# Two-layer network on one core: where the low parts of the hidden layers' activations are subtracted, and the written-out order

## The reference

```
x = layer0(x)
h = modulate(layernorm(x))
q, k, v = rope(h @ Wqkv);  x = x + gate_a * (softmax(causal(q k^T / 4)) v @ Wproj + b)
h = modulate(layernorm(x))                       # 512 x 256
z = silu(h @ w1^T * s1) * (h @ w2^T * s2)        # 512 x 1024: "up"
z = gelu(z @ h1^T * sh1)                         # 1024 -> 1024: "h1"
z = gelu(z @ h2^T * sh2)                         # 1024 -> 1024: "h2"
x = x + gate_b * (z @ w3^T * s3)                 # 1024 -> 256: "last"
```

## Time and profile before

| | |
|---|---|
| runs | 1975.2, 1977.19, 1977.64 us; median 1977.19 us |
| the profiled execution | 1979.78 us, of which the span from first to last instruction is 1978.0 us |
| mean granted PE clock | 0.971 |
| PE busy | 1856.4 us, 94% |
| DVE busy | 1375.4 us, 70% |
| ACT busy | 907.2 us, 46% |
| POOL busy | 510.0 us, 26% |

### The profile page before, as it was taken

How to read it: one execution, slowest core, us unless ns; L and a number is a source line. 1 busy time by engine, 2 the same in 40 slices (tenths; PEclk the granted TensorE clock), 3 DMA queues, 4 the chain that set the end, 5 groups by cost and what they waited for, 6 DMA issues and landing times.

```text
span 1978.0 us, 39009 instructions
## 1 busy us (share of the span) xinstructions
PE 1856.4 (94%) x15449; PEld 1293.8 (65%) x15449; DVE 1375.4 (70%) x2407; ACT 907.2 (46%) x1116; POOL 510.0 (26%) x597
## 2 busy tenths in 40 slices
PE   7998999899999998887999999999999999999998
PEld 4665657565666664444677676676776776776787
DVE  5667677766776677778768678587588678587443
ACT  2656574656565653332444524524534434534431
POOL 2434353443444342121211203102204003112120
PEclk8898999999999999888999999999999999999999
DMA  6221213221321110400122122221231231221321
GB/s 184 58 46 42 59 37 73 50 58 28 86 52 26 40 39 5 171 1 17 44 81 78 54 85 62 65 87 50 75 96 30 86 93 44 86 84 43 112 83 43
DMA packets 171812, 126.26 MB, mean 64 GB/s; under 512 B 113944, under 2 KB 148720, under 8 KB 171248
## 3 DMA queue, kind: packets, MB, share of 16 engines
q1 hardware_dynamic: 170800, 123.74, 22.6%
...
## 4 chain that ended last, share of the span: by engine, by line
PE 77%; DVE 15%; ACT 4%; issue 3%; POOL 1%; DMA 0%; SPq 0%; DVEq 0%; POOLq 0%; ACTq 0%
PE ps L2041 24%; PE ps L2025 5%; PE ps L1078 5%; PE ps L1922 4%; PE ps L1984 3%; PE ps L983 3%; PE ps L1952 3%; PE ps L2055 2%; PE ps L1108 2%; PE ps L1041 2%; PE ps L1130 2%; PE ps L1023 2%; DVE b_maxima L1689 2%; PE ps L1968 2%; PE ps L1964 2%
## 5 line engine op out<-in xcount | busy, mean ns | idle before, releaser
L2041 PE MATMUL ps<-b_acts,b_hidden_w 128*128 128x512 f32 x2048 | 504.6, 398 | 1.1 <-POOL b_acts L1616 1.1
L2041 PEld LDWEIGHTS ps<-b_acts,b_hidden_w 128*128 128x128 f32 x2048 | 376.2, 188 | 90.9 <-issue 9.8
L452 POOL TENSOR_SCALAR_AFFINE_SELECT a_probs<-a_probs 128x512 f32<-128x512 f32 (+1 forms) x224 | 166.3, 758 | 357.4 <-ACT a_probs L863 249.1
L1608 POOL TENSOR_SCALAR_AFFINE_SELECT b_work<-b_work 128x512 f32<-128x512 f32 x128 | 83.3, 663 | 673.1 <-ACT b_work L1843 673.0
L1879 ACT ACTIVATE b_acts_exact<-ps,c_s 128x512 f32<-128x512 f32 x128 | 88.2, 689 | 297.6 <-PE ps L2041 297.4
L863 ACT ACTIVATE a_probs<-ps 128x2048 f32<-128x2048 f32 (+1 forms) x96 | 153.2, 1595 | 123.5 <-DVEq L713 86.7
L1843 ACT ACTIVATE b_work<-ps 128x2048 f32<-128x2048 f32 (+1 forms) x96 | 153.4, 1597 | 90.8 <-PE ps L1968 89.0
L1689 DVE TENSOR_REDUCE b_maxima<-ps 128x4 f32<-128x2048 f32 (+3 forms) x128 | 187.9, 1489 | 3.3
L1787 DVE CAST b_acts<-b_acts_exact 128x512 fp32r<-128x512 f32 x128 | 55.8, 436 | 164.2 <-ACT b_acts_exact L1879 163.9
L1078 PE MATMUL ps<-a_probs,c_va 128*17 128x192 f32 (+4 forms) x2048 | 136.6, 388 | 2.9 <-issue 1.5
L1686 DVE TENSOR_TENSOR ps<-ps,c_causalr 128x512 f32<-128x512 f32 x128 | 86.1, 696 | 45.2 <-PE ps L1952 43.4
...
## 6 DMA issues: line engine op xcount, KB each, us to landing
b_hidden_w<-turned_h SPq DMA_DIRECT2D x128, 512.0 KB, 3.5
a_raw_next<-in_L_ffn_h_w SPq DMA_DIRECT2D x512, 16.0 KB, 1.8
...
```

The lines of the kernel that those rows point to most:

```text
L452: return nc.gpsimd.affine_select(out=z, in_=z, compare_op=ALU.is_ge, fill=0.0, base=0, pattern=[[0, blocks_n], [1, cols]], channel_multipl ...
L2041: ins = nc.tensor.matmul(here, view(hidden_w[:, m, k]), view(src[:, k, i]), start=(k + i == 0), stop=(k == NHID - 1 and i == 1))
```

## The change

Two things are edited. First, the subtraction of the low part of every hidden tile (`h1` and `h2`, 128 in all) moves from DVE to POOL. DVE's copy now adds to a new semaphore `h_high`; POOL waits for that count, subtracts, and adds to `h_split`. DVE's wait for its own copy goes. Second, `ORDER` is replaced by another order of the same 1750 entries: the first 357 entries and the last 53 (from `last.6.1.1` on) are the same, and what lies between is shuffled locally. In layer 0 no step changes; only its place in the order does.

```diff
@@ ORDER @@
-0:xT.2.1 0:lv.13.0 0:lin.14.0 0:lv.13.1 0:again.14 0:win.13.0 0:lh.12 0:r.2.0 0:lv.13.2 0:win.13.1 0:lv.14.0 0:win.14.0 0:norm.4 0:wv.13.0 0:kk.2.0
...
-1:h2.1.6.0 1:max.3.1.1 1:turn.2.1 1:h2.1.6.1 1:h2.1.7.0 1:max.3.1.2 1:h2.1.7.1 1:out.2.0 1:att.3.0.0 1:out.2.1 1:last.1.0.0 1:att.3.0.1 1:values.3.0.0
...
+1:max.3.1.0 1:heads.2.3 1:h2.1.5.1 1:h2.1.6.0 1:max.3.1.1 1:turn.2.1 1:h2.1.6.1 1:h2.1.7.0 1:again.3.0 1:max.3.1.2 1:h2.1.7.1 1:out.2.0 1:att.3.0.0
+1:out.2.1 1:last.1.0.0 1:att.3.0.1 1:values.3.0.0 1:last.1.0.1 1:xT.2 1:last.1.1.0 1:att.3.0.2 1:split.2 1:tq.3.2 1:last.1.1.1 1:up.2.0.0 1:tk.3.2
...
@@ second_layer @@
     h_split = sem("gelu_split")
+    h_high = sem("gelu_high_ready")
@@ gpsimd @@
                 nc.gpsimd.tensor_tensor(act_a[:, i, 1], exact_a[:, i], act_a[:, i, 0].bitcast(F32), ALU.subtract).then_inc(a_ready, 1)
+            elif name in ("h1", "h2") and step[3]:
+                m = step[2]
+                z, dst = (exact_a[:, m], act_a[:, m]) if name == "h2" else (exact_b[:, m], act_b[:, m])
+                pool.wait_ge(h_high, (b * 2 + (name == "h2")) * NHID + m + 1)
+                nc.gpsimd.tensor_tensor(dst[:, 1], z, dst[:, 0].bitcast(F32), ALU.subtract).then_inc(h_split, 1)
@@ vector @@
                 dve.wait_ge(gelu_ready, (b * 2 + (name == "h2")) * NHID + m + 1)
-                link(nc.vector.tensor_copy(dst[:, 0], z))
-                nc.vector.tensor_tensor(dst[:, 1], z, dst[:, 0].bitcast(F32), ALU.subtract).then_inc(h_split, 1)
+                nc.vector.tensor_copy(dst[:, 0], z).then_inc(h_high, 1)
```

More of the change, by code:

```diff
@@ L1236 @@
[L1236 to L1239, removed]
@@ L1252 @@
[L1252 to L1255, removed]
@@ L1256 @@
[L1256 to L1267, removed]
@@ L1304 @@
-1:h1.4.5.0 1:att.5.3.2 1:values.5.3.0 1:values.5.3.1 1:norm.6 1:h1.4.5.1 1:hT.6 1:h1.4.6.0 1:values.5.3.2 1:h1.4.6.1 1:proj.6.0 1:proj.6.1 1:h1.4.7.0
-1:h1.4.7.1 1:proj.6.2 1:proj.6.3 1:h2.4.0.0 1:h2.4.0.1 1:h2.4.1.0 1:tq.6.0 1:h2.4.1.1 1:tk.6.0 1:h2.4.2.0 1:max.6.0.0 1:h2.4.2.1 1:tk.6.1 1:h2.4.3.0
-1:heads.5.3 1:max.6.0.1 1:h2.4.3.1 1:tq.6.1 1:h2.4.4.0 1:max.6.0.2 1:h2.4.4.1 1:h2.4.5.0 1:max.6.1.0 1:h2.4.5.1 1:h2.4.6.0 1:max.6.1.1 1:turn.5.1
-1:h2.4.6.1 1:h2.4.7.0 1:again.6.0 1:max.6.1.2 1:out.5.0 1:h2.4.7.1 1:att.6.0.0 1:out.5.1 1:last.4.0.0 1:att.6.0.1 1:values.6.0.0 1:last.4.0.1
@@ new lines @@
+0:win.30.0 0:lv.30.0 0:xT.6.0 0:lh.29 0:pair.31 0:wh.29 1:norm.0 0:lv.30.1 0:again.31 0:win.30.1 0:xT.6.1 0:win.31.0 0:lv.30.2 0:wv.30.0 0:win.31.1
+0:fold.31 1:hT.0 0:kk.6.0 1:proj.0.0 0:wv.30.1 1:proj.0.1 1:proj.0.2 1:proj.0.3 0:wh.30 0:kk.6.1 0:wv.31.0 0:wv.31.1 0:lin.31.0 1:tq.0.0 0:lin.31.1
+1:tk.0.0 0:lin.31.2 0:flag.0 0:lh.30 1:tk.0.1 1:max.0.0.0 0:lv.31.0 1:tq.0.1 0:lv.31.1 0:lv.31.2 1:max.0.0.1 1:max.0.0.2 1:max.0.1.0 1:again.0.0
+0:r.6.0 1:max.0.1.1 0:r.6.1 0:last.6.0 1:att.0.0.0 0:last.6.1 1:att.0.0.1 0:wh.31 0:lh.31 0:turn.7.0 1:max.0.1.2 0:turn.7.1 1:values.0.0.0 0:turn.7.2
@@ new lines @@
+1:att.0.0.2 1:again.0.1 1:values.0.0.1 1:att.0.1.0 1:stats.1 0:turn.7.3 1:values.0.0.2 1:tq.0.2 1:att.0.1.1 1:tk.0.2 1:values.0.1.0 1:max.0.2.0
+0:out.7.0 1:att.0.1.2 1:tk.0.3 1:max.0.2.1 1:tq.0.3 1:max.0.2.2 1:heads.0.0 1:max.0.3.0 1:values.0.1.1 1:again.0.2 1:values.0.1.2 1:max.0.3.1
+0:out.7.1 1:att.0.2.0 1:att.0.2.1 1:max.0.3.2 1:values.0.2.0 0:xT.7.0 1:att.0.2.2 1:again.0.3 1:values.0.2.1 1:att.0.3.0 1:heads.0.1 0:xT.7.1
+1:values.0.2.2 1:ga.0 1:att.0.3.1 1:values.0.3.0 1:turn.0.0 1:att.0.3.2 1:values.0.3.1 1:norm.1 1:heads.0.2 1:values.0.3.2 1:hT.1 0:kk.7.0 1:heads.0.3
@@ new lines @@
+1:proj.1.0 1:proj.1.1 1:turn.0.1 1:proj.1.2 1:proj.1.3 0:r.7.0 0:kk.7.1 1:tq.1.0 1:out.0.0 1:tk.1.0 1:max.1.0.0 1:tq.1.1 1:max.1.0.1 1:out.0.1
+1:tk.1.1 1:max.1.0.2 0:r.7.1 0:last.7.0 1:xT.0 1:again.1.0 0:last.7.1 1:att.1.0.0 1:split.0 1:max.1.1.0 1:up.0.0.0 1:up.0.0.1 1:values.1.0.0
+1:att.1.0.1 1:up.0.1.0 1:up.0.1.1 1:att.1.0.2 1:max.1.1.1 1:tk.1.2 1:tq.1.2 1:values.1.0.1 1:max.1.1.2 1:up.0.2.0 1:again.1.1 1:max.1.2.0 1:up.0.2.1
+1:values.1.0.2 1:up.0.3.0 1:att.1.1.0 1:up.0.3.1 1:up.0.4.0 1:att.1.1.1 1:heads.1.0 1:up.0.4.1 1:max.1.2.1 1:values.1.1.0 1:up.0.5.0 1:max.1.2.2
@@ new lines @@
+1:proj.2.1 1:heads.1.3 1:proj.2.2 1:proj.2.3 1:turn.1.1 1:h2.0.0.0 1:h2.0.0.1 1:h2.0.1.0 1:tq.2.0 1:h2.0.1.1 1:tk.2.0 1:h2.0.2.0 1:max.2.0.0
+1:h2.0.2.1 1:h2.0.3.0 1:max.2.0.1 1:tq.2.1 1:h2.0.3.1 1:h2.0.4.0 1:max.2.0.2 1:h2.0.4.1 1:tk.2.1 1:h2.0.5.0 1:max.2.1.0 1:h2.0.5.1 1:h2.0.6.0
+1:max.2.1.1 1:again.2.0 1:h2.0.6.1 1:h2.0.7.0 1:max.2.1.2 1:out.1.0 1:h2.0.7.1 1:att.2.0.0 1:out.1.1 1:last.0.0.0 1:att.2.0.1 1:last.0.0.1
+1:values.2.0.0 1:att.2.0.2 1:values.2.0.1 1:again.2.1 1:xT.1 1:split.1 1:ga.2 1:last.0.1.0 1:tq.2.2 1:att.2.1.0 1:last.0.1.1 1:tk.2.2 1:up.1.0.0
@@ new lines @@
+1:up.2.7.1 1:h1.2.0.0 1:max.3.3.1 1:turn.3.0 1:h1.2.0.1 1:h1.2.1.0 1:max.3.3.2 1:h1.2.1.1 1:h1.2.2.0 1:att.3.2.2 1:again.3.3 1:h1.2.2.1 1:h1.2.3.0
+1:stats.4 1:values.3.2.2 1:att.3.3.0 1:h1.2.3.1 1:h1.2.4.0 1:att.3.3.1 1:values.3.3.0 1:h1.2.4.1 1:h1.2.5.0 1:att.3.3.2 1:values.3.3.1 1:norm.4
+1:h1.2.5.1 1:heads.3.2 1:hT.4 1:values.3.3.2 1:h1.2.6.0 1:proj.4.0 1:proj.4.1 1:h1.2.6.1 1:proj.4.2 1:h1.2.7.0 1:proj.4.3 1:h1.2.7.1 1:h2.2.0.0
+1:tq.4.0 1:h2.2.0.1 1:tk.4.0 1:h2.2.1.0 1:tk.4.1 1:max.4.0.0 1:h2.2.1.1 1:tq.4.1 1:ga.3 1:h2.2.2.0 1:max.4.0.1 1:h2.2.2.1 1:heads.3.3 1:h2.2.3.0
@@ new lines @@
+1:max.4.0.2 1:h2.2.3.1 1:h2.2.4.0 1:max.4.1.0 1:again.4.0 1:h2.2.4.1 1:h2.2.5.0 1:max.4.1.1 1:h2.2.5.1 1:h2.2.6.0 1:h2.2.6.1 1:h2.2.7.0 1:max.4.1.2
+1:turn.3.1 1:h2.2.7.1 1:att.4.0.0 1:out.3.0 1:out.3.1 1:att.4.0.1 1:values.4.0.0 1:last.2.0.0 1:att.4.0.2 1:tq.4.2 1:last.2.0.1 1:xT.3 1:again.4.1
+1:last.2.1.0 1:tk.4.2 1:split.3 1:values.4.0.1 1:max.4.2.0 1:values.4.0.2 1:last.2.1.1 1:up.3.0.0 1:att.4.1.0 1:heads.4.0 1:up.3.0.1 1:up.3.1.0
+1:att.4.1.1 1:up.3.1.1 1:up.3.2.0 1:max.4.2.1 1:values.4.1.0 1:up.3.2.1 1:values.4.1.1 1:up.3.3.0 1:att.4.1.2 1:max.4.2.2 1:up.3.3.1 1:tk.4.3
@@ new lines @@
+1:h2.3.0.0 1:proj.5.3 1:h2.3.0.1 1:h2.3.1.0 1:tq.5.0 1:h2.3.1.1 1:tk.5.0 1:h2.3.2.0 1:max.5.0.0 1:h2.3.2.1 1:tq.5.1 1:h2.3.3.0 1:max.5.0.1 1:h2.3.3.1
+1:ga.4 1:tk.5.1 1:h2.3.4.0 1:max.5.0.2 1:heads.4.3 1:h2.3.4.1 1:h2.3.5.0 1:again.5.0 1:max.5.1.0 1:h2.3.5.1 1:h2.3.6.0 1:max.5.1.1 1:turn.4.0
+1:h2.3.6.1 1:h2.3.7.0 1:max.5.1.2 1:turn.4.1 1:h2.3.7.1 1:att.5.0.0 1:out.4.0 1:out.4.1 1:att.5.0.1 1:values.5.0.0 1:last.3.0.0 1:att.5.0.2 1:tq.5.2
+1:last.3.0.1 1:xT.4 1:again.5.1 1:last.3.1.0 1:tk.5.2 1:values.5.0.1 1:ga.5 1:split.4 1:max.5.2.0 1:values.5.0.2 1:last.3.1.1 1:up.4.0.0 1:att.5.1.0
@@ new lines @@
+1:values.5.3.0 1:h1.4.4.1 1:heads.5.2 1:h1.4.5.0 1:att.5.3.2 1:values.5.3.1 1:norm.6 1:h1.4.5.1 1:h1.4.6.0 1:values.5.3.2 1:hT.6 1:heads.5.3
+1:h1.4.6.1 1:proj.6.0 1:proj.6.1 1:proj.6.2 1:turn.5.1 1:proj.6.3 1:h1.4.7.0 1:h1.4.7.1 1:h2.4.0.0 1:tq.6.0 1:h2.4.0.1 1:tk.6.0 1:h2.4.1.0 1:max.6.0.0
+1:h2.4.1.1 1:tq.6.1 1:h2.4.2.0 1:max.6.0.1 1:h2.4.2.1 1:h2.4.3.0 1:tk.6.1 1:max.6.0.2 1:h2.4.3.1 1:h2.4.4.0 1:max.6.1.0 1:h2.4.4.1 1:h2.4.5.0
+1:max.6.1.1 1:h2.4.5.1 1:again.6.0 1:h2.4.6.0 1:max.6.1.2 1:h2.4.6.1 1:h2.4.7.0 1:h2.4.7.1 1:att.6.0.0 1:out.5.0 1:out.5.1 1:att.6.0.1 1:values.6.0.0
@@ new lines @@
+1:h2.5.5.1 1:h2.5.6.0 1:max.7.1.1 1:h2.5.6.1 1:turn.6.1 1:h2.5.7.0 1:again.7.0 1:max.7.1.2 1:ga.6 1:out.6.0 1:h2.5.7.1 1:att.7.0.0 1:out.6.1
+1:last.5.0.0 1:att.7.0.1 1:values.7.0.0 1:last.5.0.1 1:att.7.0.2 1:tq.7.2 1:xT.6 1:split.6 1:tk.7.2 1:last.5.1.0 1:again.7.1 1:max.7.2.0
+1:values.7.0.1 1:values.7.0.2 1:last.5.1.1 1:up.6.0.0 1:att.7.1.0 1:heads.7.0 1:up.6.0.1 1:up.6.1.0 1:ga.7 1:att.7.1.1 1:up.6.1.1 1:up.6.2.0
+1:max.7.2.1 1:values.7.1.0 1:up.6.2.1 1:values.7.1.1 1:up.6.3.0 1:att.7.1.2 1:max.7.2.2 1:tk.7.3 1:up.6.3.1 1:up.6.4.0 1:again.7.2 1:values.7.1.2
```

146 lines of the change are left out of this document (67 added, 79 removed).

## The result

The changed kernel takes 1968.47 us (median of 6 runs, 1965.59 to 1970.79) where the kernel before takes 1977.47 (6 runs, 1975.2 to 1982.04). The ratio is 0.995, with a 95% interval of 0.9937 to 0.9964: faster by 9 us, half a per cent, clear of noise. The forecast was no change, 1978 us. The measured time lies in the range of 1965 to 1990, but on the side that had 0.29.

What follows compares the result with a forecast made beforehand. PE, busy 94%, was taken to bound the kernel. Certain terms 0 + 0.25 + 0.65 = +0.9 us on the profiled 1979.8 gave 1980.7; with the median 2.6 us lower, 1978 us was forecast, range 1965 to 1990.

Steps and rivals of the forecast that it cites:

- The order: Layer 0, junction and batches: new order keeps PE's work and nearly the same places; 0 taken, bound 7 us either way.
- the likeliest way for the whole to be wrong: Sign against the order step: the first three stages end more than 4 us earlier or later.
- Rival 2: Outside hidden stretches: new order brings maxima's work forward, closing half of 16.5 us of gaps; 1970 us, chance 0.29.
- DVE is relieved: Hidden stretches: DVE loses some 93 us, but PE is full there with 1.2 us idle; worth 0.
- POOL is loaded: Hidden tiles: 128 subtractions of 1.289 us add 165 us to POOL, which keeps up; low parts come 0.65 us later.
- Who waits for a low part: First output tile of the product after each hidden product: PE waits only at the last two batches' ends, 0.25 and 0.65 us.
- (a): From h1 to h2: later low part covered by 0.6 us, so 0; uncovered, up to 0.65 us each, 8 times at most.
- (b): From h2 to `last`: batches 0 to 5 covered; batch 6 loses 0.2 us, 0.25 with the semaphore.
- (c): Batch 7, h2 to `last`: nothing lies between, PE already waits for the low part; +0.65 us on the path.
- What stands behind the new wait on POOL: Masks, inverse roots and `ga` queue behind POOL's wait for DVE's cast; 0 taken, other bound 9.0 us.
- rival 3: Batch turns: a mask, `ga` or root comes one POOL subtraction later, costing 9.9 us; 1987 us, chance 0.21.
- The shared port: POOL's subtractions hold up DVE's hidden casts by 0.17 us each, 22 us in all, off the path; 0 in the sum.

Runs made afterwards that it cites:

- order alone: Kernel before with only ORDER replaced, subtractions staying on DVE: 1965.87 us, ratio 0.9924; run again 1963.76 us, 0.9922.
- new order of the steps to 788 alone: Kernel before with the first 788 entries in the new order, the rest old, subtractions on DVE: 1970.57 us, ratio 0.9949.
- steps behind 907: Kernel before with only the entries from 908 on (the batches) in the new order, subtractions on DVE: 1976.03 us, ratio 0.9983.
- move alone: Kernel before with the hidden subtractions moved to POOL and the old order kept: 1982.14 us, ratio 1.0012.
- its repeat: The changed kernel, unaltered, measured once more on one chip with the second run of the order alone: 1966.68 us, ratio 0.994 to the kernel before.
- the kernel with `ga.1` first: Changed kernel with batch 1's gate addition on POOL put ahead of batch 0's last h1 tile: 1965.37 us, ratio 0.9936 to the kernel before.
- the kernel with the last ones on DVE: Changed kernel with the last of each eight low parts subtracted on DVE, with its own semaphore: 1969.57 us, ratio 0.994 to the kernel before.

## Why the prediction was wrong

**The failed step is "The order".** It read "Value taken: 0, the row being silent on the sign". The order alone gives 15 us, twice the bound of 7 us that a tenth of the idle time in the first stages had set. Three things were wrong in it. The tenth was a guess: in the stages that it was taken from, the new order of the steps to 788 alone wins 0.0051, 10 us, of their 49.4 + 18.6. The bound looked at no idle time in the batches, where the orders differ as well and the steps behind 907 win 3.4 us. And an order moves more than idle time: PE's busy time fell too, through the clock for one. Counting which step names are neighbours could show none of this. The text did name this step as "the likeliest way for the whole to be wrong", with the sign of it: stages ending over 4 us earlier; the first hidden product starts 11.8 us earlier. How much of this one trace can tell is another matter: in its two traces the order alone starts that product at 961.0 and at 952.5.

**Rival 2 had the result, not the whole reason.** It gave 1970 for an order that closes gaps outside the hidden stretches. That the number fits is in part luck: it expected half of the 16.5 us of gaps in the batches to close, waits on maxima above all. PE's waits on maxima fell from 4.5 + 3.4 us to 2.4 + 3.3, by 2.2 us:

```profile
PE ps L1957 <- ACTq L1851: 4.7, 4, 1.2
PE ps L1969 <- DVE b_maxima L1695: 3.3, 4, 1.6
PE ps L1957 <- DVE b_maxima L1695: 2.4, 1, 2.4
```

Of these 1.8 came back as waits on ACT's queue, 4.7 us in place of 2.9. Nor does the order need the lighter DVE: it is faster with the heavy one. Whether it could have been found without planning for a lighter DVE, no run can say.

**"DVE is relieved": right.** The relief is worth nothing. Batch 1's hidden stretch is full after as it was before, 96.00 of 96 us, with DVE at 59.1 in place of 68.4 us:

```profile
1093.00:1189.00 96.00, 96.00 (x591) 70.74 (x588) 59.09 (x104) 39.03 (x45) 28.30 (x26) 1.00 0.30 88
```

The 89.4 us have become idle time of DVE. The line of its additions of the causal mask, for one, waits for PE's scores for 61.3 us where the order alone has 36.0 (groups of the changed kernel, then of the order alone):

```profile
L1692 DVE TENSOR_TENSOR ps<-ps,c_causalr 128x512 f32<-128x512 f32 x128 | 86.2, 696 | 63.1 <-PE ps L1957 61.3
```

```profile
L1685 DVE TENSOR_TENSOR ps<-ps,c_causalr 128x512 f32<-128x512 f32 x128 | 86.1, 695 | 37.9 <-PE ps L1951 36.0
```

**"POOL is loaded" and "Who waits for a low part": right.** The source view of the new POOL line:

```profile
L1622 POOL TENSOR_TENSOR b_acts<-b_acts_exact,b_acts x128: 1263/1287/1401, 959.2 to 1951.7; 128x512 fp32r<-128x512 f32 x128
...
  PEld ps L2060: 1.4, 2
  PE ps L2060: 0.9, 1
```

128 of 1.287 us (1.289 forecast), and nobody waits for them but `last`, in batches 6 and 7. None of the hidden products L2046 does, so (a), h1 to h2, is covered. (b), the end of batch 6's h2, forecast 0.25:

```profile
1867.28 8.24 PE L2060 MATMUL ps<-b_w3T,b_acts 128*128 128x256 f32 x64
...
1867.92 1.29 POOL L1622 TENSOR_TENSOR b_acts<-b_acts_exact,b_acts 128x512 fp32r<-128x512 f32 x1 [0.96 <-DVE b_acts L1793]
...
1869.27 6.05 PEld L2060 LDWEIGHTS ps<-b_w3T,b_acts 128*128 128x128 f32 x50 [0.27 <-POOL b_acts L1622]
```

The weight load waits 0.27 us, and the 64 products take 8.24 us where they took 7.92: 0.32. (c), the last batch: 0.92 - 0.30 = 0.62 for 0.65.

**"What stands behind the new wait on POOL": not settled, and rival 3 too high.** Taken at 0 with 9.0 as the other bound. The move costs 2.4 us in the old order; that less the 0.9 of (b) and (c) leaves 1.5, within the noise. In the new order the difference of the change and the order alone is 3.6 to 5 us, of which (b) and (c) explain 0.9 us and the waits for rotated tiles 0.6. Masks, the sign that was named, do not show it: in the changed kernel no wait of PE on a mask is listed from 960 to 1908 us. What the queue does shift is `ga`, by some 50 us in the move alone.

**"The shared port": the price did not come where it was looked for.** The forecast put 0.17 us on each cast, up to 22 us, off the path. The casts' mean is what it was, 432 ns (436 before, from 55.8 us over 128):

```profile
L1793 DVE CAST b_acts<-b_acts_exact 128x512 fp32r<-128x512 f32 x128 | 55.2, 432 | 196.9 <-ACT b_acts_exact L1884 196.5 <-DVE b_meanvar L1649 0.2
```

In front of its own subtraction POOL is waiting for the cast, so these two cannot meet. What met was `ga`, pushed by subtractions, with other work of DVE: with a rotation's sum, 0.82 us late (the prediction had named these sums, at up to 1.29 us each), and in the move alone with the cast of maxima, 0.43 us.

**Left open.** First, the rest of the move's price in both orders. One thing goes with it in the new one. In the batches there are short stretches in which PE's granted clock falls to half, 1.2 of 2.4 GHz (one is shown in the last section). Three are in each of the changed kernel, its repeat and the kernel with `ga.1` first, with PE busy for 980.1 to 980.4 us from first to last hidden product; two are in both runs of the order alone and in the kernel with the last ones on DVE, with 978.0 to 978.3 us. What one stretch is worth can be read where the order is the same: 981.6 us before, with three, against 980.5 in the move alone, with two, so about 1.1 us. That is half of the 2 us; the other half stays unexplained, and no run set the number of such stretches by itself. Second, why the junction up to the first `up` is quicker in the changed kernel, its repeat and the one with `ga.1` first (156.5 to 157.7 us) than in the order alone, twice, before, the move alone and the kernel with the last ones on DVE (159.8 to 160.7), though no moved subtraction runs before 959 us. Third, which swaps in each part of the order do the work.
